# The passage from the attention half to the feed-forward half: batch 0 prepared within the last attention batch, its up products set between the steps of the attention tail, and the response matrix finished a batch later

## What is computed

```python
# first layer
x = _ln(src) * (1.0 + scale) + shift
scores = jnp.einsum('bhqd,bhkd->bhqk', q / math.sqrt(HEAD_DIM), k)
scores = scores + attention_bias
scores = jnp.where(src_mask, -jnp.inf, scores.astype(jnp.float32))
probs = jax.nn.softmax(scores, axis=-1).astype(v.dtype)
ctx = jnp.einsum('bhqk,bhkd->bhqd', probs, v)
x = x + (ctx @ Wo + bo)
h = _ln(x) * g2 + beta2
ff = _gelu2(h @ W1 + b1) @ W2 + b2
# second layer, on x + ff
U_o = gram_schmidt(U)
V_o = gram_schmidt(V)
basis = U_o @ V_o.T
pooled = hidden_states.mean(axis=1)
h1 = jax.nn.relu(pooled @ gate_w1.T + gate_b1)
base_act = jax.nn.sigmoid(h1 @ gate_w2.T + gate_b2)
strength = (base_act * mod * knob)[:, None, :]
proj = hidden_states @ basis
feats = proj @ basis.T[:, :R]
response = feats @ resp_w.T + resp_b + safety_bias
return hidden_states + strength * response
```

## Time and profile before

| | us |
|---|---|
| median of 3 runs | 1368.19 |
| lowest, highest | 1367.77, 1368.98 |
| the profiled execution | 1369.96 |
| its span, first to last instruction | 1367.8 |

### The profile page before, as it was taken

One profiled execution on the slowest core, in us unless ns is written; L12 is line 12 of the kernel. 1 busy time (PEld: TensorE's weight loads), 2 busy tenths in 40 slices (PEclk: granted clock), 3 DMA queues, 4 the chain that ended last, 5 costly groups with the idle time before them and its releaser, 6 DMA issues. The chain is left out here.

```text
span 1367.8 us, 39618 instructions
## 1 busy us (share of the span) xinstructions
PE 1321.2 (97%) x11936; PEld 1119.3 (82%) x11936; DVE 1075.3 (79%) x3638; ACT 1071.8 (78%) x2664; POOL 871.5 (64%) x874
## 2 busy tenths in 40 slices
PE   4999999999999999999999998789999999999997
PEld 3777777777777777777777776579999999999997
DVE  4777777787877777778778777578888888888885
ACT  1788888888888888888888886777777777777773
POOL 4999989989999998998999998311222222122210
PEclk9999999999999999999999999989999999999998
DMA  9546656555564665655556482101010110111100
GB/s 289 184 152 200 191 161 207 166 188 181 169 210 152 197 191 159 208 164 187 181 169 210 154 259 70 32 24 40 31 46 31 35 42 31 46 31 41 36 24 32
DMA packets 182670, 175.07 MB, mean 128 GB/s; under 512 B 15552, under 2 KB 182112, under 8 KB 182624
## 3 DMA queue, kind: packets, MB, share of 16 engines
q1 hardware_dynamic: 181248, 173.64, 40.1%
q10 hardware_dynamic: 1376, 0.85, 0.2%
HBM read 157.69 MB, written 16.78 MB: 128 GB/s over the span
## 5 line engine op out<-in xcount | busy, mean ns | idle before, releaser
L428 POOL TENSOR_TENSOR ring<-ring,maskv 128x1024 f32<-128x1024 f32 x256 | 600.0, 2373 | 12.4 <-DMA ring<-in_fside 5.1
L912 ACT ACTIVATE ring<-ring,nmax 128x256 f32<-128x256 f32 x1024 | 452.5, 501 | 24.6 <-DVE nmax L606 24.6
L606 DVE CUSTOM_DVE_ANT_0 ring<-bank,ring 128x256 f32<-128x256 f32 x1024 | 373.0, 418 | 90.4 <-PE bank L1176 73.5
L917 ACT ACTIVATE pT<-bank 128x512 f32<-128x512 f32 x416 | 239.5, 592 | 103.5 <-PE bank L1191 103.4
L1191 PE MATMUL bank<-ident,ring 128*128 128x128 f32 x2048 | 292.6, 278 | 1.4 <-ACT pT L917 1.1
L1191 PEld LDWEIGHTS bank<-ident,ring 128*128 128x128 f32 x2048 | 231.9, 143 | 70.6 <-issue 47.9
L1047 ACT ACTIVATE work<-bank,b1t 128x256 f32<-128x256 f32 x256 | 107.6, 476 | 109.0 <-PE bank L1390 109.0
L1176 PE MATMUL bank<-work 32*128 32x256 f32 x2048 | 148.4, 404 | 6.0 <-DVE nmax L606 5.2
L1390 PE MATMUL bank<-hT_high,w_high 128*128 128x256 f32 x512 | 147.9, 289 | 3.4 <-DVE hT_rest L781 3.4
L1403 PE MATMUL bank<-w_high,gT_high 128*128 128x256 f32 x512 | 148.1, 289 | 0.0
L1403 PE MATMUL bank<-w_rest,gT_high 128*128 128x256 f32 x512 | 145.3, 284 | 0.0
(11 more groups left out here) (162 smaller groups left out, 2730.5 us busy)
## 6 DMA issues: line engine op xcount, KB each, us to landing
ring<-in_fside SPq DMA_DIRECT2D x128, 1024.0 KB, 7.7
xt<-in_x SPq DMA_DIRECT2D x32, 256.0 KB, 3.2
x_d<-x2s SPq DMA_DIRECT2D x32, 256.0 KB, 7.8
work<-x_d SPq DMA_DIRECT2D x32, 256.0 KB, 2.8
out<-pT SPq DMA_DIRECT2D x32, 256.0 KB, 2.2
mk<-in_mask SPq DMA_DIRECT2D x32, 64.0 KB, 6.7
w<-in_W SPq DMA_DIRECT2D x2, 1024.0 KB, 10.5
wada<-in_W_ada SPq DMA_DIRECT2D x1, 512.0 KB, 8.1
```

Of the source, the lines that this page charges most:

```text
L428: nc.gpsimd.tensor_tensor(v, v, m, ALU.add).then_inc(s_masked, 1)
L606: nc.vector.tensor_tensor_reduce(out=v, in0=score_ps[h % HG][:, qt], in1=v, scale=-1.0, scalar=ROW_MAX_NEG, op0=ALU.add, op1=ALU.min, accu ...
L912: nc.scalar.activation(v, v, ACT.Exp, bias=nmax[:, b.par, h, qt:qt + 1], scale=-1.0).then_inc(s_exp, 1)
L917: nc.scalar.activation(pT[:, h % (2 * HG)], tp_ps[h % 2], ACT.Copy).then_inc(s_pta, 1)
```

## The change

Batch 0 is prepared within attention batch 31: its x2 is loaded at batch 29, `stats2(0)` and the whole split of w1 (copy and rest, both on DVE now) stand in DVE's batch 31, `inv_std2(0)` on POOL, `yn_out(0)` and `hT_out(0)` on ACT and `y_transpose(0)` on PE between the last transposes. The tail of batch 31 is taken out of the loop body and its steps alternate with the four `up_pair` steps of batch 0. The w2 split, `yn_out(1)`, `hT_out(1)`, and the gates of batch 0 stand between them on ACT and DVE. The response matrix's first step follows the last `project_o`; its second and third stand in `body2` of batch 1. Scratch buffers are laid out anew so that the early buffers do not overlap what attention still reads.

```diff
@@ SP @@
+            def load_y(b):
+                sp.wait_ge(s_x2st[b.par], 16 * b.half + 16)
+                sp.dma_start(y2[:, b.par], x2_d[bass.ds(b.n, 1)].rearrange("a (t p) d -> p (a t) d", p=P)).then_inc(s_y[b.par], 16)
             def body(b, n):
...
                 if n == B - 3:
                     for dst, src, loaded in loads_rest:
                         sp.dma_start(dst, src).then_inc(loaded, 16)
+                    load_y(Batch(0))
+                    load_y(Batch(1))
...
-            sp.wait_ge(s_qk, NG * B)
-            load_y(Batch(0))
-            load_y(Batch(1))
             store_x2(Batch(B - 2))
             store_x2(Batch(B - 1))
             sp.wait_ge(s_pv, NG * B)
@@ POOL @@
-            run_batches(pool, 0, 3, B - 3, B + 1, body)
+                if n == B - 1:
+                    inv_std2(Batch(0))
+            run_batches(pool, 0, 3, B - 3, B, body)
+            gs_norm(B - 1)
+            inv_std2(Batch(1))
+            gs_update(B - 1)
+            add_b2(Batch(0))
@@ DVE @@
+            def split_up_weights():
+                dve.wait_ge(s_tp, H * (B - 1))
+                nc.vector.tensor_copy(w1s[0], w1[:]).then_inc(s2_wd, 1)
+                dve.wait_ge(s2_wd, 1)
+                nc.vector.tensor_tensor(w1s[1], w1[:], f32(w1s[0]), ALU.subtract).then_inc(s2_wl, 1)
...
+                    if n == B - 1:
+                        stats2(Batch(0))
+                        split_up_weights()
                     copy_pT(b, 11)
...
-            stats2(Batch(0))
-            body(Batch(B), B)
-            x2_out(Batch(B - 1))
-            hT_rest(Batch(0))
-            split_weights(1)
+            zero, last = Batch(0), Batch(B - 1)
+            hT_rest(zero)
+            x2_out(Batch(B - 2))
+            gs_reciprocal(B - 1)
+            stats2(Batch(1))
+            normalise_ctx(last, 0)
+            gate_pair(zero, 0)
+            normalise_ctx(last, 1)
+            gate_pair(zero, 1)
+            gT_rest(zero, 0)
+            down_weights_rest()
+            gate_pair(zero, 2)
+            gT_rest(zero, 1)
+            hT_rest(Batch(1))
+            gate_pair(zero, 3)
+            x2_out(last)
+            response_matrix(0)
+            gT_rest(zero, 2)
+            stats2(Batch(2))
...
                 if main:
                     gate_pair(b, 0)
                 if tail:
                     gT_rest(b.plus(-1), 3)
                 if tail2:
                     hidT_rest(b.plus(-2))
+                if n == 1:
+                    response_matrix(1)
+                    response_matrix(2)
+                    response_rest()
@@ ACT @@
+                    exp_head(b, 15)
+                    if n == B - 1:
+                        yn_out(Batch(0))
+                    copy_pT(b, 12)
+                    copy_pT(b, 13)
...
+                    copy_pT(b, 14)
+                    if n == B - 1:
+                        hT_out(Batch(0))
+                    copy_pT(b, 15)
...
+            pv_out(last, 2)
+            pv_out(last, 3)
+            gs_coefficients(B - 1)
+            zero = Batch(0)
+            tanh_pair(zero, 0)
+            gs_write(B - 1)
             yn_out(Batch(1))
+            tanh_pair(zero, 1)
+            act.wait_ge(s_tp, H * B)
+            gT_high(zero, 0)
+            ctxT_out(last)
+            down_weights_high()
+            tanh_pair(zero, 2)
+            gT_high(zero, 1)
+            hT_out(Batch(1))
+            tanh_pair(zero, 3)
+            gT_high(zero, 2)
+            yn_out(Batch(2))
...
                     tanh_pair(b, 0)
                 if tail:
                     gT_high(b.plus(-1), 3)
+                if n == 1:
+                    response_high()
@@ PE @@
                 if prep:
                     x_back(b.plus(1), True)
+                if n == B - 1:
+                    pe.wait_ge(s_gii, B)
+                    y_transpose(Batch(0))
                 if main:
                     transposes(b, 15)
                     pv(b, 2)
...
+            pv(last, 3)
+            pe.wait_ge(s_reduced, 2 * H * B)
+            up_pair(zero, 0)
+            ctx_natural(last, 0)
+            up_pair(zero, 1)
+            ctx_natural(last, 1)
+            up_pair(zero, 2)
+            ctx_transpose(last, False)
+            y_transpose(Batch(1))
+            up_pair(zero, 3)
+            project_o(last, False)
+            response_matrix(0)
...
                 if main:
                     up_pair(b, 0)
+                    if n == 1:
+                        response_matrix(1)
                     up_pair(b, 1)
+                    if n == 1:
+                        response_matrix(2)
```

## The result

The change makes the kernel slower. The kernel after takes 1377.99 us, the median of four executions (1377.09 to 1379.89); the kernel before, run beside it, takes 1368.09. The ratio is 1.0069, with a 95% interval of 1.0055 to 1.0083. The profiled execution of after took 1377.09 with a span of 1374.9.

What follows compares the result with a forecast made beforehand. PE bounds the second half without idle time, so its late start there is paid in full: early gains are lost in batch 1, 1368.19 + 10.0 = 1378.2 us. Forecast's own range 1375 to 1382; full range 1371 to 1384.

Steps and rivals of the forecast that it cites:

- Part 1: Batch 31: DVE's `stats2(0)` and w1 split, 4.9 us, delay head 11's copy; PE waits 4.7 at head 13, then half clock.
- Part 2: Batch 31: `pv(31, 2)` waits for `x2_out(30)`, behind `hT_rest(0)`, `hT_out(0)` and PE's `y_transpose(0)`; starts 11.0 us late, at 889.9.
- Part 3: Passage between the halves: `up_pair(0, 0)` at 892.6, 6.3 us early; through ACT's queue `up_pair(1, 0)` at 905.4, 3.9 early.
- Part 4: Batch 1: late load and `stats2(2)` delay `yn_out(2)`; PE idles 7.5 us before third response step; `down(0, 0)` 10.0 late.
- From there to the end: After batch 1's `down(0, 0)`: PE has the same work without idle time, so nothing more is lost or regained.
- the terms named for the upper one: Additions to the forecast: upper bound of DVE's w1 copy, +1.2 us, and low clock in the first pairs, +1.5.
- (a): Rival: PE's clock stays high behind the long waits in batches 31 and 1; 1373 us, chance 0.10.
- (b): Rival: not slower, batch 2's statistics are ready before ACT needs them near 906; 1365.8 us, chance 0.10.
- (c): Rival: w1's copy takes 2.7 us, first pairs run at half clock, or delay reaches batch 2; 1382 to 1386, chance 0.12.

Runs made afterwards that it cites:

- e1: Kernel after with one DVE line moved: `x2_out(30)` ahead of `hT_rest(0)` again; 1376.17 us, ratio 1.0060.
- e3: Kernel after with batch 2's x2 loaded ahead of `store_x2(31)` and `stats2(2)` ahead of `hT_rest(1)` on DVE; 1371.04 us, ratio 1.0025.
- e10: e6 with three orders put back as in after: load behind `store_x2(31)`, `stats2(2)` last, `x2_out(31)` behind `hT_rest(1)` and `gate_pair(0, 3)`; 1364.53 us.
- e9: e6 with the weight splits put back: w1's on DVE in batch 31, w2's on ACT and DVE; 1368.49 us, ratio 1.0001.
- e7: Kernel after with the edits of e1 and e3 together; 1368.01 us, ratio 0.9994 to before.
- e8: Kernel after once more, unchanged, beside e5 to e7; 1375.23 us, ratio 1.0056.
- e5: Kernel after with 52 unread matmuls before PE's third response step, filling most of the wait; 1375.21 us, ratio 1.0045.
- e2: Kernel after with head 11's copy on DVE ahead of `stats2(0)` and w1's split; 1378.01 us, ratio 1.0071.
- e4: Kernel after with the second and third response steps and their copies moved from batch 1 to batch 2; 1377.59 us, ratio 1.0072.
- e6: The better order: kernel after with both splits on POOL, e1's and e3's orders, `x2_out(31)` earlier, other steps and response steps re-placed; 1356.45 us, ratio 0.9908.
- e11: e6 once more, unchanged, beside e9 and e10; 1356.67 us, ratio 0.9918.

## Why the prediction was right

The forecast was 1378.2 and the median is 1377.99; the span was forecast at 1377.8 and is 1374.9. That the medians agree to 0.2 us is luck: the second sample of the same kernel has 1375.23, and the steps below miss by up to 2.3 us and make each other good. What is right is the direction, the size within some 3 us, and the chain of waits. The steps, one by one:

**Part 1, the insertion: right in place, too large.** DVE's row of steps after:

```profile
874.40 0.74 DVE L693 BATCH_NORM_STATS2 st6b<-work 128x6 f32<-128x256 f32 x2
875.24 0.25 DVE L701 BATCH_NORM_AGGREGATE mvb<-st6b 128x2 f32<-128x6 f32 x2
875.41 1.19 DVE L707 CAST w_high<-w 128x2048 fp32r<-128x2048 f32 x1
876.63 2.29 DVE L709 TENSOR_TENSOR w_rest<-w,w_high 128x2048 fp32r<-128x2048 f32 x1
878.84 0.68 DVE L618 COPY pT<-bank 128x512 f32<-128x512 f32 x1
```

4.4 us instead of 4.9, the statistics and the subtraction as taken. The copy takes 1.19, and I had taken 1.5 from a row of DVE that ran beside POOL's mask additions. The Trainium skill's two results per cycle for a copy within SBUF ("VectorE: DVE Perf Modes", section "Mode 2×_2P — use both read ports for one tensor"), by which the estimate was 1.1, comes nearer than that row. PE waited 4.02 us, where 4.7 was said, and then ran at half clock: 0.50 from 880 to 882, but 0.85 already from 882 to 884. That low stretch was some 3.7 us long, not 6.5. With part 2 they make `pv(31, 2)` 8.7 us late, where 11.0 was said (887.65 against 889.9). The 0.44 us for a head's four transposes is not what the earlier trace rows show, where eight take 1.12 from start to start; but the 0.9 at half clock came true in head 13 (0.91).

**Part 2, the wait for `x2_out(30)`: right.** 2.91 us, said 2 to 3, by the releaser that was named; e1 removes it by that order alone.

**Part 3: right, with one error that made good another.** `up_pair(0, 0)` came at 891.1, said 892.6. `pv(31, 3)` and the first pair ran at half clock, which stood in the range only (1 to 1.5 us), and so `up_pair(1, 0)` came at 904.47, 0.9 before the 905.4 that was said.

**Part 4, the chain in batch 1: right in each link.** `x2_out(31)` ended at 906.65 (said 907.4), the statistics began at 910.08 (910.8), `yn_out(2)` at 912.95 (913.6), the third step at 917.24 (917.9) after 7.56 us (7.5), and `down(0, 0)` ended near 924.5 (925.5): each 0.7 to 1.0 early, by what part 3 had left over. e3 takes this chain out of the kernel after, and it is worth 4 to 7 us there; e10 puts it into the better order, with a later `x2_out(31)`, and it costs 7.9.

**From there to the end: right, but not tested to a microsecond.** The forecast had the second half unchanged. From the first `hid_transpose` to the end of the span before took 446.6 us (1367.8 less 921.23), after 444.7 (1374.9 less 930.24). From 1350 to 1360 before had a granted clock of 0.89 and after one of 1.00:

```profile
1350.00:1360.00 10.00, 8.29 (x60) 0.89 0.01 2
```

```profile
1350.00:1360.00 10.00, 8.26 (x70) 1.00 0.08 26
```

From 1340 to 1350 it was 0.94 and 1.00. The windows don't hold the same work, so this is no exact account, but it goes with a span that grew by 7.1 only, with a passage 9.2 longer. Over the other kernels that do the same work in it this stretch takes 444.5 to 447.4. The longest are those where the granted clock fell near the end, 447.4 in e9 and 447.1 in e10 (0.84 from 1340 to 1350) and 446.7 in e1 (0.83 from 1350 to 1360); with 1.00 in both windows it takes 444.7 (e3), 444.8 (e7) and 444.9 (e8).

**The range.** Its own bounds run from 1375 to 1382; the terms named for the upper one (1.2 and 1.5) reach 1380.9 only. The measured time turns on neither.

**The rivals.** (a), a clock that stays high, fell: 0.50 stands behind all three waits of 4.02, 2.91 and 7.56 us in after. Behind the 2.91 it came late or not at all: `pv(31, 2)` itself ran at full clock (1.07), and in e8 so did `pv(31, 3)`. The rule that DVE's copies between matmuls do not cool PE (the Trainium skill, "TensorE: Matmul & The Clock Gate", section "Loop structure matters more than you think") did not save this case, since PE here stands idle for the copy. Its price, set at 3.2 us behind the long wait, was 2 to 3 (e5). (b) fell: the statistics came at 910, not near 906. (c) happened in one of its three parts, the half clock in the first pair, and was balanced by part 1. The right total rests on that in part: taken alone, part 1 was 2.3 us too dear.

**Not foreseen.** POOL's small steps were held up (e2), so `yn_out(0)` began at 880.07 only. In after this is hidden behind the gap before head 13; it is the reason that e2 gains nothing.

## What to carry to other kernels

Where hand-written queues are interleaved, follow each moved step through every queue until it meets the bound engine again: the passage began 7.8 us earlier and still lost, in large part because one load was issued behind a store that waits for the last result, and one engine's next step waited for that load. Where such a delay surfaces is not where it is made (e4): undo the order at the head of the chain, here an early load and an early statistic, worth 4 to 7 us of the kernel after. And put long copies on the engine whose work has ended, even if it is the slower one, as the splits on POOL show: w1's take 6.5 us there against 3.5 on DVE, and the kernel is some 12 us faster than with both splits back on DVE and ACT.

## What the runs showed of the hardware

**DVE and POOL hold each other up.** POOL's instruction on two elements per partition took 0.19 us on its own and 2.26 beside DVE's subtraction. The first two rows are `inv_std2(0)`, beside DVE's w1 split shown above, the last is the same step of batch 2:

```profile
875.66 0.99 POOL L435 TENSOR_SCALAR vpeb<-mvb 128x2 f32<-128x2 f32 x1 [9.14 <-DVE mvb L701]
876.72 2.26 POOL L436 TENSOR_SCALAR mnegb<-mvb 128x2 f32<-128x2 f32 x1
...
911.66 0.19 POOL L436 TENSOR_SCALAR mnegb<-mvb 128x2 f32<-128x2 f32 x1
```

The other way round, in before, a DVE step on eight elements beside POOL's mask additions:

```profile
839.71 2.32 DVE L678 TENSOR_SCALAR b1t<-b1c 128x8 f32<-128x8 f32 x1
```

The small instruction ends as the long one beside it ends: in after at 876.65 and 878.98, where DVE's copy ends at 876.60 and its subtraction at 878.92. e9 and e6 test this: two other small steps of POOL, on the Gram-Schmidt norms, took 1.54 and 1.67 us in e9 beside DVE's split of w1, and 0.68 and 0.19 in e6, where DVE has no split. The Trainium skill, "GPSIMD Engine Reference", section "1. Specifications", says that POOL shares its way into SBUF with VectorE, and contends with VectorE's instructions that use two ports or have two inputs in SBUF; these rows agree.

**The low clock is not of one length.** The wait in batch 30 is the same in both kernels (4.61 us), yet the clock was low for some 6.5 us behind it in before, and back to 1.00 from 852 in after, where PE resumed at 848.85: some 3 us. Behind the 4.02 us before head 13 it was some 3.7, and in e3 about 10, from 905.8 on, though PE was busy 8.90 of the 10 us from 906 to 916. Nor does it begin with the wait: in e3 PE had run at full clock for 1.4 us behind 2.95 us of idle time before it fell, and in after `pv(31, 2)` ran at full clock behind 2.91 and `pv(31, 3)` at half. Single executions of one kernel differ by microseconds (after 1373.66 to 1379.89, before 1365.40 to 1371.12, e6 and e11, with no wait over 1.4 us in the passage, 1355.60 to 1359.13), which puts a limit on what any sum over such a passage can tell. That the clock alone makes this spread is not shown, and what sets the length of the low stretch stays open.
